# A ring of five x halves, the residual in place, and a new order of one turn's work

## The reference

```
xn  = layernorm(x)                                # over 256 columns
Q, K, V = xn @ Wq + bq, xn @ Wk + bk, xn @ Wv + bv, in 16 heads of 16
Qp, Kp  = relu(normalised(Q or K) @ projection) + 0.1      # 64 features per head
attn = (Qp @ (Kp^T V)) / max(Qp . sum(Kp), 1e-6);  attn @ Wo + bo
ffn  = top-2 of 8 experts on xn: silu(xn @ w1) @ w2, gates from a softmax of xn @ router,
       rows beyond an expert's capacity dropped
out  = x + attn + ffn + xn
```

## Time and profile before

| | us |
|---|---|
| median of 3 runs (lowest, highest) | 1437.63 (1431.65, 1439.33) |
| the profiled execution, its own time | 1448.41 |
| its span | 1446.8 |
| PE, DVE, ACT, POOL busy | 1250.6, 792.5, 663.7, 802.3 |
| turns 0 to 7 and what leads to them | the first 686.4 |
| the experts' part | the rest, 760.4 |
| a turn in the middle, from 357.6 to 435.9 | 78.3, of which PE is busy 62.2 |

### The profile page before, as it was taken

One profiled execution on the slowest core, in us unless ns is written; L12 is line 12 of the kernel. 1 busy time (PEld: TensorE's weight loads), 2 busy tenths in 40 slices (PEclk: granted clock), 3 DMA queues, 4 the chain that ended last, 5 costly groups with the idle time before them and its releaser, 6 DMA issues.

```text
span 1446.8 us, 38172 instructions
## 1 busy us (share of the span) xinstructions
PE 1250.6 (86%) x14334; PEld 997.8 (69%) x14334; DVE 792.5 (55%) x1830; ACT 663.7 (46%) x1140; POOL 802.3 (55%) x804
## 2 busy tenths in 40 slices
PE   4886877878796968644999999999999999999997
PEld 2555554545555545423888888888888888888886
DVE  6676858586767677653433434344444434344442
ACT  3766766666766666631323323232323333232322
POOL 3637382846556473861256656555555556565553
PEclk9798787979797978856999999999999999999999
DMA  2223232322413232504864444444544444344451
GB/s 84 98 73 111 89 118 89 118 89 75 132 45 118 89 105 66 182 25 154 275 180 82 78 77 70 75 75 74 78 75 74 77 77 77 69 77 75 78 78 15
DMA packets 156139, 133.73 MB, mean 92 GB/s; under 512 B 93825, under 2 KB 144258, under 8 KB 154946
## 3 DMA queue, kind: packets, MB, share of 16 engines
q1 hardware_dynamic: 122338, 95.58, 23.2%
q0 software_dynamic: 33632, 35.71, 15.3%
HBM read 61.83 MB, written 52.61 MB: 79 GB/s over the span
## 4 chain that ended last, share of the span: by engine, by line
PE 58%; DVE 18%; issue 7%; DMA 5%; ACT 5%; POOL 5%; SPq 1%; another core or an unknown queue 1%; ACTq 0%; DVEq 0%; POOLq 0%
PE bank L944 26%; PE bank L960 25%; DVE area L1319 4%; DMA area<-in_x_dram 4%; POOL slot_table L1046 2%; DVE area L1198 2%; DVE area L1216 1%; ACT area L559 1%; PE bank L821 1%; DVE area L1187 1%; PE bank L807 1%; ACT area L578 1%; PE bank L728 1%; PE bank L705 1%
## 5 line engine op out<-in xcount | busy, mean ns | idle before, releaser
L944 PE MATMUL bank<-area 128*128 128x256 f16 x3408 | 385.5, 273 | 20.0 <-DMA area<-xg 15.3
L960 PE MATMUL bank<-area 128*128 x3408 | 383.5, 273 | 0.0
L944 PEld LDWEIGHTS bank<-area 128*128 x3408 | 334.1, 98 | 60.4 <-issue 21.1
L1142 POOL DMA_INDIRECT out_dram<-area,mt x142 | 229.6, 1617 | 251.3 <-ACT area L647 221.8
L1468 DVE TENSOR_SCALAR area<-area 128x512 f16<-128x512 f32 x284 | 129.0, 454 | 422.0 <-ACT area L637 390.0
L960 PEld LDWEIGHTS bank<-area 128*128 128x128 f16 x3408 | 333.3, 98 | 38.7
L637 ACT ACTIVATE area<-bank 128x512 f32<-128x512 f32 x284 | 169.6, 598 | 189.3 <-PE bank L944 176.0
L1046 POOL DMA_INDIRECT slot_table<-area x128 | 128.2, 1001 | 149.3 <-PE bank L821 107.3
L647 ACT ACTIVATE area<-bank,mt 128x256 f32<-128x256 f32 x142 | 59.6, 470 | 329.5 <-PE bank L960 324.8
L1470 DVE SCALAR_TENSOR_TENSOR area<-area 128x512 f16<-128x512 f32 x284 | 196.9, 693 | 9.8
L1135 POOL DMA_INDIRECT xg<-xn_split,mt x142 | 143.5, 1010 | 44.7 <-issue 42.7
(11 more groups left out here) (172 smaller groups left out, 1457.7 us busy)
## 6 DMA issues: line engine op xcount, KB each, us to landing
area<-in_w_dram SPq DMA_DIRECT2D x32, 512.0 KB, 5.3
experts_split<-area SPq DMA_DIRECT2D x32, 512.0 KB, 4.3
area<-experts_split SPq DMA_DIRECT2D x8, 2048.0 KB, 8.1
area<-in_x_dram SPq DMA_DIRECT2D x16, 512.0 KB, 6.8
xn_split<-area SPq DMA_DIRECT2D x16, 512.0 KB, 3.0
out_dram<-area SPq DMA_DIRECT2D x32, 256.0 KB
xg<-xn_split,mt POOLq DMA_INDIRECT x142
area<-xg SPq DMA_TRANSPOSE x142
```

The lines of the kernel that those rows point to most:

```text
L944: mm = nc.tensor.matmul(big[j][:, i2 * TS:(i2 + 1) * TS], we[:, bass.ds(e * EXPERT + (k * 2048 + wl * 1024 + c * P), P)], moe_xT[t % XT][: ...
L960: mm = nc.tensor.matmul(yb[:, a * D:(a + 1) * D], hT[u % 2][:, c, hl, a * P:(a + 1) * P], we[:, bass.ds(e * EXPERT + off, D)], start=(c == ...
L1142: nc.gpsimd.indirect_dma_start(orows, bass.IndirectOffsetOnAxis(mt[:, u % GRP, a, 0:1], 0), y_sb[u % 2][:, a, :], None, bounds_check=last_ ...
```

## The change

- The two x buffers and the residual buffer become a ring of five half-batch buffers `x_half`. Half `h` of batch `b` lies in buffer (2b+h) mod 5. `resid_rows` overwrites x with the residual in the same buffer, and `out_drain` reads it there. A load may start when the half that was in its buffer five halves ago has been drained: `x_load(b+2, 0)` waits for `out3` of batch b-1, `x_load(b+2, 1)` for `out1` of batch b.
- SP issues `x_load(b+2, 0)` at the head of turn b, and `x_load(b+2, 1)` behind `out_store` 0 and 1. `w_store(b, 2)` and `w_load(b+1, 0)` move ahead of these two stores.
- DVE computes `row_sums` and `row_factors` of batch b+2 in turn b, between the two halves of `out_drain`. Before, those of batch b+1 stood near the head of turn b.
- PE runs `attend` 4 to 7 ahead of `qk_project(b+1, 0)`; `o_transpose(b, 0)` and `qk_project(b+1, 1)` come behind `v_and_squares(b+1, 0)` and ahead of `o_project(b, 0)`. DVE and ACT follow this order. `nd` has two buffers, so `constant_part` of half 1 can run early.
- DVE refines the norms of half 0 itself (10 instructions), POOL only those of half 1.
- POOL scatters all 16 slots in a row, as soon as `place` has written them. Before it waited for `ab7`, scattered 8, refined the norms of half 0, and scattered 8.
- ACT: `resid_rows(b+1, 0)` before `qk_read_half(b+1, 1)`, `resid_rows(b+1, 1)` behind `w_high(b, 3)`; before, both stood at the turn's end.

```diff
-BODY = (attn("rank", "vsum", "kvT") + prep("xT0", "xT1") + attn("cn", "ab0", "ab1", "ab2", "ab3") + prep("xT2", "xT3")
-        + attn("oT0", "oT1", "ab4", "ab5", "ab6", "ab7") + prep("v0", "v1", "nrm0", "v2", "nrmT0", "v3")
-        + attn("out0", "out1", "oT2", "oT3") + prep("v4", "v5") + attn("out2", "out3") + prep("v6", "nrm1", "v7", "nrmT1"))
+        + attn("ab4", "ab5", "ab6", "ab7") + prep("v0", "v1", "nrm0", "v2", "nrmT0", "v3") + attn("oT0", "oT1", "out0", "out1")
+        + attn("oT2", "oT3") + prep("v4", "v5") + attn("out2", "out3") + prep("v6", "nrm1", "v7", "nrmT1"))
...
+        x_half = [view([HT, D], F32) for _ in range(HALVES)]
+        def x_in(b, half):
+            return x_half[(2 * b + half) % HALVES]
...
         def x_load(sp, b, half):
-            hold(sp, resid_ready, (b - 1) * 2 + half + 1)
-            sp.dma_start(x_in[half], src).then_inc(x_loaded[half], 16)
+            n = 2 * b + half - HALVES
+            if n >= 0:
+                wait_read(sp, "attn", f"out{2 * (n % 2) + 1}", n // 2)
+            if b > 0:
+                sp.wait_ge(x_loaded[half], b * 16)
+            sp.dma_start(x_in(b, half), src).then_inc(x_loaded[half], 16)
...
         def sp_turn(sp, b, phase, x_next=True):
+            if body and x_next:
+                x_load(sp, b + 2, 0)
...
+            w_store(sp, b, 2)
+            if body:
+                w_load(sp, b + 1, 0)
             out_store(sp, b, 0)
             out_store(sp, b, 1)
-            w_store(sp, b, 2)
-            if body:
-                w_load(sp, b + 1, 0)
             if body and x_next:
-                x_load(sp, b + 2, 0)
+                x_load(sp, b + 2, 1)
             out_store(sp, b, 2)
             out_store(sp, b, 3)
-            if body and x_next:
-                x_load(sp, b + 2, 1)
...
         def act_turn(act, b, phase, first=False):
             o_hi(act, b, 1)
             if body:
-                v_copy(act, phase, b + 1, 3)
-            if body:
+                resid_rows(act, b + 1, 0)
+                qk_read_half(act, b + 1, 1, 0, 4)
                 w_high(act, b, 3)
-                qk_read_half(act, b + 1, 1, 0, 2)
+                resid_rows(act, b + 1, 1)
             oT_copy(act, phase, b, 1)
...
         def pe_turn(pe, b, phase):
                 x_transpose(pe, phase, b + 1, 1)
-                qk_project(pe, b + 1, 0, False)
-            o_transpose(pe, phase, b, 0)
             for t in range(HT, NT):
                 attend(pe, phase, b, t)
             if body:
+                qk_project(pe, b + 1, 0, False)
                 v_and_squares(pe, phase, b + 1, 0)
+            o_transpose(pe, phase, b, 0)
+            if body:
+                qk_project(pe, b + 1, 1, False)
             o_project(pe, phase, b, 0)
-            if body:
-                qk_project(pe, b + 1, 1, False)
             o_transpose(pe, phase, b, 1)
...
         def pool_turn(pool, b, phase):
-            pool.wait_ge(attn_filled, nth("attn", f"ab{NT - 1}", b))
-            scatter(pool, b, 0, 8)
-            norm_refine(pool, b + 1, 0)
-            scatter(pool, b, 8, 16)
+            scatter(pool, b)
             w_low(pool, b, 3)
             norm_refine(pool, b + 1, 1)
...
         def norms(dve, phase, b, half):
+            if half == 1:
+                rsqrt_guess(chp, ny, nsq, nu, ready=norm_guess)
+                return
+            rsqrt_guess(chp, ny, nsq, nu)
+            for step in range(3):
+                ...
...
         def out_drain(dve, phase, b, half, first):
-                v.scalar_tensor_tensor(osb[k % 2], src, 1.0 / (R_SCALE * W_SCALE), resid[:, 2 * k:2 * k + 2, :], ALU.mult, ALU.add) \
+                v.scalar_tensor_tensor(osb[k % 2], src, 1.0 / (R_SCALE * W_SCALE), x_in(b, half)[:, 2 * j:2 * j + 2, :], ALU.mult, ALU.add) \
...
         def dve_turn(dve, b, phase, first=False):
-            if body:
-                chp.start(dve, b + 1)
-                row_sums(dve, b + 1)
...
             for t in range(HT, NT):
                 attend_drain(dve, phase, b, t)
             if body:
-                qk_halves(dve, b + 1, 0, 1, 4)
+                place(dve, b, first)
+            normalise(dve, b, 0)
...
             out_drain(dve, phase, b, 0, first)
-            if body:
-                qk_halves(dve, b + 1, 1, 0, 2)
-                v_over_norm(dve, b + 1, 0, chp)
-                qk_halves(dve, b + 1, 1, 2, 3)
+            if body and b + 2 < B:
+                row_sums(dve, b + 2)
+                row_factors(dve, b + 2)
             out_drain(dve, phase, b, 1, first)
```

More of the change, by code:

```diff
@@ L33 @@
 XR = 4
+HALVES = 5
 XT = 4
@@ L216, in moe_attention @@
         rn = view([HT, 2, 8], F32)
-        nd = view([HT, H, HD + 1], F32)
+        nd = [view([HT, H, HD + 1], F32) for _ in range(2)]
         dn = view([HT, H], F32)
@@ L433, in _ @@
             for half in range(2):
-                sp.dma_start(x_in[half], xrows[half * HS:(half + 1) * HS, :].rearrange("(t p) d -> p t d", p=P)) \
-                    .then_inc(x_loaded[half], 16)
+                x_load(sp, 0, half)
             for n, w in enumerate((Wq, Wk, Wv)):
@@ L454, in _ @@
             for half in range(2):
+                x_load(sp, 1, half)
                 xs_store(sp, 0, half)
-                x_load(sp, 1, half)
                 w_load(sp, 0, half)
@@ L668, in _ @@
             last_copies(act, "first", 0)
+            for half in range(2):
+                resid_rows(act, 0, half)
             act_turn(act, 0, "body", first=True)
@@ L1021, in norm_refine @@
             g = nc.gpsimd
-            steps = [(b * 2 + half) * 13]
+            steps = [b * 13]
             def link(ins, apart=False):
@@ L1106, in _ @@
                 x_low(pool, 0, half)
-            for half in range(2):
-                norm_refine(pool, 0, half)
+            norm_refine(pool, 0, 1)
             v_total(pool, 0)
@@ L1239, in norms @@
             wait_read(dve, "prep", f"nrmT{half}", b)
-            rsqrt_guess(chp, ny, nsq, nu, ready=norm_guess)
+            if half == 1:
[3 more added lines that the diff above has]
+            for step in range(3):
+                chp.link(v.tensor_tensor(nu, nsq, ny, ALU.mult))
+                chp.link(v.scalar_tensor_tensor(ny, nu, -0.5, ny, ALU.mult, ALU.mult) if step == 2 else
+                         v.scalar_tensor_tensor(nu, nu, -0.5, ny, ALU.mult, ALU.mult))
+                chp.link(v.scalar_tensor_tensor(ny, ny, 1.5, nu, ALU.add, ALU.mult) if step == 2 else
+                         v.scalar_tensor_tensor(ny, nu, 1.5, ny, ALU.add, ALU.mult))
+            chp.link(v.tensor_scalar(norm[:, 0], ny, 1e-8 * W_SCALE, None, ALU.add))
         def v_over_norm(dve, b, half, ch):
@@ L1393, in dve_turn @@
                 attend_drain(dve, phase, b, t)
-            q_low(dve, b, 1, 0, PAIRS)
-            normalise(dve, b, 0)
-            if body:
-                place(dve, b, first)
-                qk_halves(dve, b + 1, 0, 0, 1)
-            o_low(dve, b, 0)
+            q_low(dve, b, 1, 0, 4)
             constant_part(dve, b, 1)
+            q_low(dve, b, 1, 4, PAIRS)
             for t in range(HT, NT):
@@ L1480, in _ @@
             chp.start(dve, 0)
+            cha.start(dve, 0)
             row_sums(dve, 0)
-            row_factors(dve)
+            row_factors(dve, 0)
             normalise_rows(dve, 0, 0, first=True)
@@ L1513, in _ @@
             ins.then_inc(consts_ready, 1)
-            for half in range(2):
-                qk_halves(dve, 0, half)
-                if half == 1:
-                    v_over_norm(dve, 0, 0, chp)
-                norms(dve, "first", 0, half)
-            chp.end()
+            qk_halves(dve, 0, 0)
+            norms(dve, "first", 0, 0)
+            v_over_norm(dve, 0, 0, chp)
+            qk_halves(dve, 0, 1)
+            norms(dve, "first", 0, 1)
+            row_sums(dve, 1)
+            row_factors(dve, 1)
             dve.wait_ge(bias_through, 1)
```

81 lines of the change are left out of this document (38 added, 43 removed).

## The result

| | before | changed |
|---|---|---|
| median of 6 runs, us | 1437.11 (1431.65 to 1439.33) | 1446.70 (1442.29 to 1450.61) |
| profiled execution: span, us | 1446.8 | 1443.7 |

The ratio is 1.007, 95% interval 1.0048 to 1.0091: 0.7% slower, 9.6 us. The forecast was 1452 and slower by over 0.5% had the largest chance, so sign and rough size hold, the size in part by luck, as the last part shows. But the two spans say the opposite of the medians (3.1 us shorter), and that has to be cleared up before any stretch is compared. Further down it turns out that the stall which the forecast left out isn't a matter of one profiled execution.

What follows compares the result with a forecast made beforehand. No engine was full in a turn; a chain of waits through the load of x's last half bound it. Turns 1 to 5 +16, turn 0 +9, turn 6 -2, turn 7 -8: +15 on 1437.6 gives 1452 us, range 1416 to 1500.

Steps and rivals of the forecast that it cites:

- the stall which the forecast left out: PE and DVE standing some 12 us beside 16 scatters in a row, seen in turn 7 of the kernel before.
- Stretch A: From a turn's first `k_features` to the end of its second `q_features` block: forecast to shrink from 42.2 to 34.7 us.
- The 5.3 us of the late `k_relu`: In A: gain of 5.3 us from `k_relu` no longer waiting on ACT behind `resid_rows` (4.0, plus a 2.4 wait).
- such contention at the factors: DVE's row factor steps slowed by POOL computing beside them (2.06 us for one); forecast absent in the new place.
- Stretch B: From the end of A to the next turn's `k_features`: forecast to grow from 36.0 to 45.8 us.
- The 1.0 for handoffs: 1.0 us added per turn for handoffs between engines that the list of steps leaves out.
- turns 1 to 5: Forecast 3.3 us longer each, handoffs included: +16 us together.
- The scatters: Rival: 16 scatters in a row stall B by 9 to 12 us in every turn, 1515 to 1535 us; chance 0.13.
- My test for the rival: Crawl over 8 us per turn: profiling's if the profiled run is 50 us above its median, rival's if the median follows.
- Gain: Rival: the x wait in B costs less than the one it replaces in A; 1419 us; chance 0.22.
- Row sums cost more: Rival: x lands in 8.1 us and two factor steps are slow, 4.9 us six times; 1481 us; chance 0.10.
- the change does nothing: Rival: loads still pace the turns, the wait merely moves from A to B; 1438 us; chance 0.10.

Runs made afterwards that it cites:

- short changed kernel: The changed kernel with its experts' part cut to 21 tiles in place of 71 and plain copies for transposing ones: 963.42 us (short kernel before: 926.21).
- run with the sums at the end: Changed kernel with short experts' part, row_sums and row_factors moved from between the out_drain halves to the turn's end: 969.08 us, against 963.42 without the move.
- short kernels: The kernel before and the changed kernel, both with 21 expert tiles in place of 71 and plain copies for transposing ones: 926.21 and 963.42 us.
- second set: The later set of rounds, which ran the four kernels with short experts' parts; the full kernel before had a median of 1449.86 us there.
- first set: The rounds that timed the two full kernels: medians 1437.11 us before and 1446.70 us changed; which chip they ran on isn't on record.

## Why the prediction was right, and where it wasn't

**Stretch A: the size held, one reason didn't.** 33.8 against 34.7. `q_low` came 1.5 behind `q_features`, 1.05 was forecast. The 5.3 us of the late `k_relu` are gone. But I had put them down to `resid_rows` in front of it, 4.0 and a wait of 2.4. That wait ended "remote" at 359.97, and from 354.6 on PE's own matmuls came singly; they ran in a row again from 359.73:

```profile
355.43 0.24 PE L765 MATMUL bank<-p_hl,area 32*128 32x128 f16 x2 [0.81 <-issue]
356.85 0.25 PE L765 MATMUL bank<-p_hl,area 32*128 32x128 f16 x2 [1.17 <-issue]
358.30 0.21 PE L765 MATMUL bank<-p_hl,area 32*128 32x128 f16 x1 [1.20 <-issue]
359.73 0.83 PE L765 MATMUL bank<-p_hl,area 32*128 32x128 f16 x12 [1.22 <-issue]
```

This was the stop, beside scatters 9 to 16 of before. `resid_rows` was over at 357.56, and what `k_relu` waited for came at 359.97 whether it stood there or not. So by this trace taking `resid_rows` away alone would have left `k_relu` where it was, and what freed it was that the scatters moved; no run did the one without the other. The short changed kernel agrees: it has the stop in B and only 0.7 us of "issue" waits at `k_features`. It also means that the 42.2 of before is a length with the stop in it, and that of a round without it isn't known.

**A loss in A that I didn't have.** `normalise_rows` of half 0 took 4.6 us in place of 1.4, in each of turns 1 to 6, beside the end of `v_total` and then `w_low` on POOL. The prediction looked for such contention at the factors only. There it was right: all their steps took 0.17 us, POOL idle. In the run with the sums at the end `normalise_rows` starts at 399.48, when POOL has finished both, and takes 1.37. The Trainium skill (SBUF — State Buffer, "Who interferes with whom") counts `tensor_scalar` among the operations of VectorE that can take the shared port pair, besides those with two SBUF inputs; the trace agrees, 4.63 against 1.37. I had used only the half of that rule that speaks of two inputs. What the 3.3 us cost a turn wasn't tried: ACT reaches `q_features` (L532) at 388.81, 0.85 us after PE began it, and couldn't have begun before about half of its 0.84 us, so it may be little.

**Stretch B: right in mechanism, two terms too large.** The wait sits where it was put, between the halves of `out_drain`, with PE behind at `nrm1`. Row sums and factors 6.0 (forecast 6.0), from there to the next turn 3.2 (3.2). The first drain ended after 28.8 (29.5), the load left after 29.3 (30.0) and landed in 5.4 (6.5): 1.8 us in all, B 43.9 in place of 45.8. The 1.0 for handoffs wasn't there. The load landed in 5.0 to 7.6 us over the six turns; where it took 7.6, DVE waited 8.3 and PE 5.5, where 5.4 (turn 4), 6.0 and 2.3, so the landing is a term that spreads. Over the turns: turn 0 +10.2 (forecast +9, in which I gave 0.6 to `bias_split`; PE waited 4.1 for it), turns 1 to 5 +4.0 (+16), turn 6 -4.1 (-2), turn 7 some -2 without the stop (-8), the prologue +2.1 (0). Sum +10 against +15.

**What was luck.** The sum came nearer than its terms. For turns 1 to 5, the largest term, the forecast had four times too much; 12 us were missing there, turn 7, turn 0 and the prologue put 9 back, and turn 6 took 2 more. In turn 7 the 5.3 in front of A was, by the trace of before, the stop again. And the prologue is no work of the change: in the short kernels it is the changed one that has the shorter (44.9 against 47.7), and in each of the four traces a prologue over 47 us has a granted clock of 0.96, one under 46 us a clock of 1.00.

**The scatters.** "For a part of the profiling alone speaks that the profiled execution was 10.8 us longer than the median": this step failed. By what the second set shows, the two numbers came from different rounds, one with the stop and one without. My test for the rival (the crawl in the trace, and the median with it or not) gives a split verdict: in the first set there was no crawl in the changed kernel's turns and the forecast stands, in the second there was, and the medians went with it (37.2 us apart in place of 9.6). So the rival was a real case, priced too high: 9 to 12 us a turn were forecast, 23.4 / 7 = 3.3 were found in the trace.

**The rivals.** *Gain* asked for a landing under 5 us and a drain before 27; it got 5.4 and 28.8. *Row sums cost more* and *the change does nothing* didn't come. But in turns 2 to 5 the last one describes what happened better than the forecast does: they last 313.9 us together against 313.2 before, 0.2 more a turn where 3.3 were forecast, and in turn 4 A gave 8.4 and B took 7.9: there the wait merely moved from A to B. The loss lies in turns 0 and 1 (13.5 us), of which turns 6 and 7 give some back.

**Open.** Not tried: the indirect scatters replaced by plain writes, which would show whether they bring the stop; `normalise_rows` ahead of `v_over_norm`; `w_high` and `resid_rows` behind the second `oT_copy`, for which PE waits 2.1 us a turn.

## What to carry to other kernels

A wait is worth what reaches the engine that paces the turn. Read it there (19.0 us at `nrm1`), not at the engine that stands (40.1 us on DVE). When a step is moved, follow every engine that waits for what now stands behind it, and look at what GpSimd does beside each VectorE step in its new place: a 0.2 us exponential between two relus, behind one subtraction that took 2.0 us in place of 0.17, cost more than the wait that the move saved. And when a profiled time and a median disagree, compare both in one set of rounds before calling the difference an effect of the profiler.

## What the runs showed of the hardware

- Towards the end of a row of 8 or 16 scatters by indirect DMA the other engines stop together: in turn 4 of the kernel before and of the short changed one PE for 4.4 and 4.5 us and ACT for 2.4 and 3.5, DVE with them, and longer in turn 7: 18 to 23 us of PE's "issue" waits in five traces, 5.3 in the one without the stop. The profile shows nothing that they wait for, and the cause is open. The full changed kernel had 6.6 us of such waits in seven turns in one set of rounds, its short form 32.5 in another.
- A one-input VectorE instruction, 128x256 with two per-partition factors, went from 0.34 to 1.16 us while GpSimd worked on 128x512, 128x256 and 128x1024 tensors (its L1018, L1020 and L1006), and one on 128x8 with two inputs in SBUF from 0.17 to 2.0 us or more beside GpSimd's 128x1024 addition.
- Loads of 512 KB into SBUF landed 3.7 to 7.6 us after their issue in the trace of the full changed kernel, the six that its turns wait for in 5.0 to 7.6.
